# Outer products of a recurrence on GpSimd instead of VectorE, in three of thirteen rounds

## What is computed

```python
def step(s, rkvw):                       # s: 16 x 16 per head
    r_t, k_t, v_t, w_t = rkvw
    a = k_t[..., :, None] * v_t[..., None, :]            # outer product k x v
    out = jnp.einsum('bhi,bhij->bhj', r_t, u * a + s)
    s = a + w_t[..., :, None] * s
    return (s, out)
_, out = jax.lax.scan(step, s0, rkvw)    # over the 256 tokens
```

## Time and profile before

| what | value |
|---|---|
| median of 3 runs | 2239.98 us (2239.05 to 2240.32) |
| the profiled execution's own time | 2244.5 us |
| its span, first to last instruction | 2242.8 us |
| mean granted TensorE clock | 0.933 of full speed |
| busy in the span: PE, DVE, ACT, POOL | 1972.2, 1434.6, 859.1, 523.8 us |
| round n a s c | about 1843 to 1964 us |
| round a s c | about 1964 to 2071 us |
| round s c | about 2071 to 2161 us |
| round c, to the end | about 2161 to 2243 us |

### The profile page before, as it was taken

One profiled execution on the slowest core, in us unless ns is written; L12 is line 12 of the kernel. 1 busy time (PEld: TensorE's weight loads), 2 busy tenths in 40 slices (PEclk: granted clock), 3 DMA queues, 4 the chain that ended last, 5 costly groups with the idle time before them and its releaser, 6 DMA issues.

```text
span 2242.8 us, 30164 instructions
## 1 busy us (share of the span) xinstructions
PE 1972.2 (88%) x11012; PEld 1352.9 (60%) x11012; DVE 1434.6 (64%) x2431; ACT 859.1 (38%) x2016; POOL 523.8 (23%) x248
## 2 busy tenths in 40 slices
PE   5789999999999854999998999999999998796455
PEld 4566676666665533667675766776767666564233
DVE  2366776666766430121388887787786878999951
ACT  2466676666665431222121422432423313231221
POOL 1233334334333230011020310302204103040100
PEclk9789999999999976999998999999999998888688
DMA  5000010000000005543545636447445454353321
GB/s 193 24 1 25 11 33 23 9 23 19 23 14 11 15 26 137 165 163 132 198 141 179 197 104 221 156 134 252 141 139 190 141 170 141 102 173 111 124 75 47
DMA packets 155185, 234.54 MB, mean 105 GB/s; under 512 B 24152, under 2 KB 72024, under 8 KB 155080
## 3 DMA queue, kind: packets, MB, share of 16 engines
q1 hardware_dynamic: 138184, 216.28, 29.3%
q10 hardware_dynamic: 16896, 16.80, 2.1%
HBM read 191.09 MB, written 41.96 MB: 104 GB/s over the span
## 4 chain that ended last, share of the span: by engine, by line
PE 44%; DVE 7%; ACT 3%; DMA 3%; issue 2%; SPq 2%; POOL 1%; POOLq 0%; ACTq 0%; DVEq 0%
PE b_f_bank L1511 10%; PE b_f_bank L1501 9%; PE b_a_bank L1534 8%; PE b_c_bank L1544 6%; PE b_a_bank L1553 4%; DVE b_ring L1739 3%; PE b_c_bank L1534 2%; PE b_y_bank L1573 2%; DVE b_ring L1728 1%; DMA b_o<-b_o_all 1%; PE b_c_bank L1553 1%; PE b_f_bank L1655 1%; DVE b_ring L1746 1%; POOL b_mixed L1417 1%; SPq L1348 0%
## 5 line engine op out<-in xcount | busy, mean ns | idle before, releaser
L299 POOL TENSOR_TENSOR a_prob<-a_prob,a_rowinv 128x1024 f32<-128x1024 f32 x128 | 242.4, 1894 | 511.0 <-DVE a_rowinv L657 510.9
L1739 DVE TENSOR_TENSOR_SCAN b_ring<-b_ws,b_ring 128x1028 f32<-128x1028 f32 x128 | 352.2, 2792 | 6.0 <-ACT b_ring L1951 3.1
L823 ACT ACTIVATE a_prob<-a_score,a_low 128x256 f32<-128x256 f32 x512 | 253.6, 497 | 246.7 <-DVE a_low L649 246.7
L1417 POOL TENSOR_TENSOR b_mixed<-b_mixed,b_xaT 128x1024 f32<-128x1024 f32 x40 | 120.0, 3000 | 620.9 <-DVE b_mixed L1756 620.9
L1511 PE MATMUL b_f_bank<-b_w_ring,b_f1T 128*128 128x512 f32 x512 | 240.2, 619 | 12.0 <-DMA b_w_ring<-in_w_dram 6.6
L1501 PE MATMUL b_f_bank<-b_hTf,b_w_ring 128*128 128x256 f32 x1024 | 236.4, 387 | 12.8 <-ACT b_xaT L1931 5.4
L1501 PEld LDWEIGHTS b_f_bank<-b_hTf,b_w_ring 128*128 128x128 f32 x1024 | 195.3, 193 | 48.9 <-issue 19.9
L649 DVE CUSTOM_DVE_ANT_0 a_score<-a_score,a_fill 128x256 f32<-128x256 f32 x512 | 196.6, 448 | 5.0 <-DVE a_score L636 0.2
L1788 DVE TENSOR_TENSOR b_xf<-b_f_bank,b_xf 128x512 f32<-128x512 f32 x64 | 44.0, 688 | 223.1 <-PE b_f_bank L1511 223.1
L636 DVE SCALAR_TENSOR_TENSOR a_score<-a_S,a_mask 128x1024 f32<-128x1024 f32 x128 | 150.8, 1220 | 51.9 <-PE a_S L435 51.9
L1511 PEld LDWEIGHTS b_f_bank<-b_w_ring,b_f1T 128*128 128x128 f32 x512 | 99.2, 198 | 130.8 <-issue 120.0
(11 more groups left out here) (155 smaller groups left out, 2960.9 us busy)
## 6 DMA issues: line engine op xcount, KB each, us to landing
b_w_ring<-in_w_dram SPq DMA_DIRECT2D x64, 1024.0 KB, 5.4
b_vs<-b_v_all SPq DMA_DIRECT2D x32, 512.0 KB, 6.2
b_shared<-in_Wv_dram SPq DMA_DIRECT2D x8, 1024.0 KB, 6.1
b_shared<-in_Wk_dram SPq DMA_DIRECT2D x8, 1024.0 KB, 5.6
b_shared<-in_Wg_dram SPq DMA_DIRECT2D x8, 1024.0 KB, 7.6
b_shared<-in_Wo_dram SPq DMA_DIRECT2D x8, 1024.0 KB, 8.8
b_shared<-in_Wfv_dram SPq DMA_DIRECT2D x8, 1024.0 KB, 6.7
b_shared<-in_Wfk_dram SPq DMA_DIRECT2D x8, 1024.0 KB, 5.9
```

The costliest lines, as they stand in the source:

```text
L299: nc.gpsimd.tensor_tensor(two, two, inv.to_broadcast([P, 2 * TT, SEQ]), ALU.mult)\
L823: last = nc.scalar.activation(prob[:, slot, a * SEQ:(a + 1) * SEQ], score[:, slot, a * SEQ:(a + 1) * SEQ], ACT.Exp, bias=low[:, head, a:a ...
L1417: nc.gpsimd.tensor_tensor(mixed[:, f % 2, :, :], mixed[:, f % 2, :, :], xaT[:, :, 1:SEQ + 1], ALU.add)\
L1739: last = nc.vector.tensor_tensor_scan(x_, flat(ws[:, :, :]), x_, 0.0, ALU.mult, ALU.add)
```

## The change

The product of a step is put into a function of its own, `outer_product`, that takes the engine. In rounds that have a stage s and no stage f (the last three with s) POOL calls it for all eight steps, at places in its own order written out by hand, and DVE's `step` leaves it out. In all other rounds DVE issues it as before. The waits are the same as before, on the engine that now issues the product. The cut diff:

```diff
+        def outer_product(engine, eng, s, u):
+            if u == 0:
+                eng.wait_ge(k_in.sem, k_in.at(s, 1))
+            if u % (STEPS // V_PARTS) == 0:
+                eng.wait_ge(vs_in[u * V_PARTS // STEPS].sem, vs_in[u * V_PARTS // STEPS].at(s, 1))
+            eng.wait_ge(y_summed.sem, y_summed.at(s, max(u - 1, 0)))
+            alone(eng)
+            engine.tensor_tensor(ring[:, u % 2, :, :, 1:SEQ + 1],
+                                 ks[:, :, :].unsqueeze(1).to_broadcast([P, JCOLS, IROWS, SEQ]),
+                                 vs[:, u // 2 % 2, u % 2 * JCOLS:(u % 2 + 1) * JCOLS, :].unsqueeze(2)
+                                 .to_broadcast([P, JCOLS, IROWS, SEQ]), ALU.mult).then_inc(kv_made.sem, 1)
@@ POOL, body
+                def products(*us):
+                    if s is not None and f is None:
+                        for u in us:
+                            outer_product(nc.gpsimd, pool, s, u)
+                products(0, 1)
                 ... o plus bonus; add_xa(a, 2)
+                products(2)
                 ... xf (only with f); add_xa(a, 3)
+                products(3)
                 ... o times its norm; add_xa(a, 4)
+                products(4)
                 ... sx of n
+                products(5)
                 ... sx2 of c
+                products(6, 7)
                 ... add_xa(n, 0); add_xa(n, 1)
@@ DVE
-            def step(s, u):
+            def step(s, u, own_product=True):
                 slot = ring[:, u % 2, :, :, :]
-                ... the waits and the product
+                if own_product:
+                    outer_product(nc.vector, dve, s, u)
                 dve.wait_ge(kv_made.sem, kv_made.at(s, u + 1))
@@ DVE, body, for each u from 0 to 7
-                    step(s, u)
+                    step(s, u, f is not None)
```

More of the change, by code:

```diff
@@ L1797, in body @@
                 if s is not None:
-                    step(s, 0)
+                    step(s, 0, f is not None)
                 if n is not None:
@@ L1805, in body @@
                 if s is not None:
-                    step(s, 1)
+                    step(s, 1, f is not None)
                 if a is not None:
@@ L1809, in body @@
                 if s is not None:
-                    step(s, 2)
+                    step(s, 2, f is not None)
                 if c is not None:
@@ L1821, in body @@
                 if s is not None:
-                    step(s, 3)
+                    step(s, 3, f is not None)
                 if c is not None:
@@ L1853, in body @@
                 if s is not None:
-                    step(s, 4)
+                    step(s, 4, f is not None)
                 if c is not None:
@@ L1865, in body @@
                 if s is not None:
-                    step(s, 5)
+                    step(s, 5, f is not None)
                 if f is not None:
@@ L1878, in body @@
                 if s is not None:
-                    step(s, 6)
+                    step(s, 6, f is not None)
                 if l is not None:
@@ L1884, in body @@
                 if s is not None:
-                    step(s, 7)
+                    step(s, 7, f is not None)
                 if f is not None:
```

## The result

The changed kernel takes 2299.09 us (median of 4, 2297.65 to 2300.58) against 2239.52 us before (median of 4, 2238.24 to 2240.32). The ratio is 1.0267, with a 95% interval of 1.0249 to 1.0284: slower by 59.6 us. The forecast was 2290 in a range of 2262 to 2308.

What follows compares the result with a forecast made beforehand. It took DVE as the bound or nearly so in the three rounds; 17.5 + 17.9 + 16.4 = 51.8 us on a 2240 median gave 2291.8, stated as 2290, range 2262 to 2308.

Steps and rivals of the forecast that it cites:

- The turns: POOL and DVE: a POOL product meeting a scan or weighing costs DVE 4.2 us instead of 2.28, +1.92.
- Product 0: Before a round's first scans, exposed: +2.4 us in n a s c, scans 4.4 later in a s c, +1.2 in s c.
- round s c: Third of the three changed rounds: forecast +16.4 us.
- Product 1 and the addition of the bonus: Product 1 falls in step 0, +4.2 us; no extra cost was forecast for the addition.
- round a s c: Second of the three changed rounds: forecast +17.9 us.
- Shift 3, o times g: Shift 3 late by 6.0 and 6.9 us; from its end to o times g 17.1 us instead of 12.9.
- Product 5: Ahead of z in n a s c, +1.9 us; in a s c 3.0 and s c 2.1 instead of 2.28.
- Products 6 and 7: Product 6 holds c's mixes by 4.2 us; product 7 delays step 7's scans, starting 20.9 us after the mixes.
- Round c: The last round, behind the three changed ones: keeps its 82 us, no change.
- round n a s c: First of the three changed rounds: forecast +17.5 us.
- A rival mispriced: Products don't hold DVE: 21 products times 2.28 saved, less waits, 36 us faster, 2204; chance 0.06.

Runs made afterwards that it cites:

- memset run: The changed kernel with each POOL product replaced by three memsets that read nothing, those products left out of the computation: 2237.8 us, ratio 0.9997.
- extra-turn run: The kernel before, DVE keeping its products, plus 24 POOL tensor_tensor of 128x2048 on unused tensors at the changed kernel's places: 2328.82 us, ratio 1.0397.
- norm-first run: The changed kernel with product 3 behind o times its norm on POOL instead of ahead of it: 2286.4 us, ratio 1.0203.
- last run: Memsets on POOL replace products 1 to 6 only, product 3's behind o times its norm; products 0 and 7 are DVE's: 2231.6 us, ratio 0.9964.

## Why the prediction was right, and where it wasn't

**The turns: right.** The profile of before showed them in 1024-element additions only; the product of 2048 holds DVE for 4.14 us, against 4.2 taken. Of the 24, products 0 and 7 of each round were exposed instead (39.2 us of idle), and 18 met DVE: the excess over the memset run is 22.5 us on the scans, 29.2 on the weighings (90.8 against 61.6), and the rest on L1875 (c's mixes), L1792 (norms) and L1865 (z), about 74 in all, which is 18 times 4.14. The memset run removes it and the whole loss with it; the extra-turn run keeps it without the saving and came out at 2328.8 for 2328 expected.

**Product 0: right in the two longer rounds.** 7.0 us after the start of each the scans begin, as worked out (1850.2 less 1843.3, 1971 less 1964). In round s c they begin 2.1 us later than before, not 1.2. Alone, product 0 costs 7.8 us in the three rounds.

**Product 1 and the addition of the bonus: missed.** I let this addition cost the same as before. It had run beside a norm (1.85 us) or beside shift 2 from PSUM (0.6 us in round a s c). It now stands behind products 0 and 1 and falls into the scans of step 0 (10.78 us is 4.49, 4.14 and 2.15). In a s c this is 1.5 us more.

**Shift 3, o times g: right.** The idle before shift 3 fell to 1.6 and 1.9 us. From shift 3's end to o times g it took 17.1 us, the number forecast; the wait behind product 3 is the 4.34 us that the norm-first run took away.

**Product 5: missed in a s c.** I gave it 3.0 us, with part of it beside L1860 (g). It fell whole on the norm L1792, which lasted 5.18 instead of 1.00 us: 1.2 us more. With the above this is the 2.9 us by which round a s c was short.

**Products 6 and 7: right.** The two mixes were held by 4.2 us, and step 7's scans waited for PE's sums and then for POOL, 6.9 us of idle (8.7 in round s c). In round s c it was 0.9 us longer in sum than forecast; PE ran the product with Wfr in 9.16 us there, before in 8.66.

**Round c: missed.** I kept its 82 us; it took 2.7 more with the same instructions. Up to o times g it is 3.1 us longer: 1.4 because the DMA ended later that POOL's addition of the bonus waits for (it began 14.4 us into the round, before 13.0), and 1.6 because the matmuls of the head variance took 3.61 us instead of 1.97. PE's granted clock in the round fell from 0.76 to 0.72. These matmuls in round c before, after, in the extra-turn run and in the last run:

```profile
2180.07 1.97 PE L1553 MATMUL b_c_bank<-b_sq,b_mean_head 128*128 128x256 f32 x8 [1.27 <-ACT b_o L2024]
2233.24 3.61 PE L1577 MATMUL b_c_bank<-b_sq,b_mean_head 128*128 128x256 f32 x8 [1.27 <-ACT b_o L2040]
2262.52 1.96 PE L1589 MATMUL b_c_bank<-b_sq,b_mean_head 128*128 128x256 f32 x8 [1.27 <-ACT b_o L2053]
2161.99 3.75 PE L1593 MATMUL b_c_bank<-b_sq,b_mean_head 128*128 128x256 f32 x8 [1.27 <-ACT b_o L2057]
```

It would be natural to blame DVE's longer rounds, which leave PE idle for longer ahead of round c. The runs speak against it: the extra-turn run has the longest rounds of all (406 us for the three, before 316) and the short matmuls, and the last run has the shortest (304) and the long ones. PE's idle time ahead of the head matmuls was 15.5, 16.0, 15.3 and 14.8 us in these four. The duration goes with the granted clock of the round: 0.72 to 0.74 in the five traces where these matmuls are long, 0.75 to 0.77 in the nine where they are short. What decides between the two is open, and so is whether the 2.7 us belong to the change at all: round c took between 77.6 and 81.4 us in the traces of all runs.

**The size.** 51.8 forecast, 58.6 in the trace: 2.9 from a s c, 1.1 from s c, 2.7 from c. By medians it is 59.6. That round n a s c hit 17.5 is in part luck, two errors of 0.6 us that cancel: its mixes came 13.4 us later than before where 14.0 was forecast, and step 7's scans began 21.5 us after them where 20.9 was.

**A rival mispriced.** If products didn't hold DVE I gave 2204, 36 us faster. The memset run, which is that rival made real, gives 2237.8, and without exposed products 2231.6. What failed is the step "21 products times 2.28": I took DVE for the bound throughout, as its busy share of 91, 96 and 99% suggested, and saw only two gaps before PE. Behind DVE's order PE's is nearly as long. So with POOL's 4.5 us a product the move had some 7 us to win in the places tried, even without turns. A faster second engine was not tried.

## What to carry to other kernels

Before an elementwise instruction is moved from VectorE to GpSimd, look for collisions that the trace already has: a GpSimd instruction that lasts twice its shortest, or a VectorE one longer by a GpSimd duration. If they take turns, the move pays only beside VectorE instructions that read PSUM or while VectorE idles, and a wait that puts it exactly there (behind the weighing, ahead of sums from PSUM) is worth more than starting early. And price the gain by what comes next: an engine that is 95% busy can still be only a few us ahead of the engine that it feeds.

## What the hardware showed that wasn't expected

A GpSimd instruction that only writes doesn't take part in the turns (a weighing beside memsets took 2.29 us). A tensor_scalar with one SBUF tensor as input, two per-partition scalars and an SBUF output does (L1792, 5.18 us instead of 1.00), while statistics with one SBUF input don't (1.29 us beside a product). For the weighing and the memsets this agrees with the Trainium skill, SBUF — State Buffer, section "Who interferes with whom": a VectorE instruction with two SBUF inputs contends with a GpSimd instruction that reads SBUF, and not with one that only writes it. For the statistics it agrees too, since the page frees instructions with one SBUF input outside the 2-port modes. The tensor_scalar fits the page only if it ran in such a mode, which the page says this operation can enter; no row names the mode, but 512 elements took 0.54 us, where the statistics took 0.69.

The eight matmuls of the head variance take 1.97 us in some rounds and 3.5 to 3.8 in others, with the same pause of 1.27 us ahead of them.
